# Softmax sums by half the products with ones: key tiles added in pairs on GpSimd, and value products moved among the thirds of Q and K

## The reference, cut to what matters

```
att = einsum('bhqd,bhkd->bhqk', q, k) * (1.0 / sqrt(hs))
att = where(causal, att, -inf)
att = softmax(att, axis=-1)
y = einsum('bhqk,bhkd->bhqd', att, v)
```

## Time and profile before

| what | value |
|---|---|
| median of three runs | 1278.62 us (1278.06 to 1281.37) |
| profiled execution, its time | 1269.57 us |
| its span | 1267.7 us |
| PE busy, share | 93% |
| DVE, ACT, POOL busy, share | 54%, 36%, 19% |
| mean granted clock of PE | 0.968 |
| M(1), first of the steps M that the change can move | 76.35 us |
| M(14) | 389.92 us |

### The profile page before, as it was taken

How to read it: one execution, slowest core, us unless ns; L and a number is a source line. 1 busy time by engine, 2 the same in 40 slices (tenths; PEclk the granted TensorE clock), 3 DMA queues, 4 the chain that set the end, 5 groups by cost and what they waited for, 6 DMA issues and landing times.

```text
span 1267.7 us, 20196 instructions
## 1 busy us (share of the span) xinstructions
PE 1183.1 (93%) x6404; PEld 935.7 (74%) x6404; DVE 686.9 (54%) x1469; ACT 456.2 (36%) x699; POOL 240.8 (19%) x370
## 2 busy tenths in 40 slices
PE   7788999999999879994999999999999999999996
PEld 5565676576575558883688888899999997778885
DVE  5564656656557546664447634343444442666744
ACT  3254435334435322222343334244444433333331
POOL 2021314413414410003100440000000000433200
PEclk8989999999999979997999999999999999999998
DMA  7336573532524222225223666245345531666440
GB/s 241 86 100 238 179 249 118 133 88 51 150 61 125 80 85 83 84 76 157 101 82 93 208 227 199 79 149 175 122 145 172 171 99 53 206 178 195 144 139 33
DMA packets 129277, 169.72 MB, mean 134 GB/s; under 512 B 17553, under 2 KB 70801, under 8 KB 129169
## 3 DMA queue, kind: packets, MB, share of 16 engines
q1 hardware_dynamic: 115360, 136.64, 35.2%
q0 software_dynamic: 8496, 28.32, 6.7%
q10 hardware_dynamic: 5312, 3.42, 1.2%
HBM read 95.98 MB, written 47.19 MB: 113 GB/s over the span
## 4 chain that ended last, share of the span: by engine, by line
PE 74%; DVE 8%; SPq 5%; POOL 3%; DMA 3%; issue 3%; ACT 2%; ACTq 1%; POOLq 0%; DVEq 0%
PE routed_ps L819 18%; PE routed_ps L1370 16%; PE psT L471 11%; SPq L354 5%; PE chosen_psG L819 4%; PE chosen_psY L819 4%; PE routed_ps L1389 2%; PE routed_ps L1390 2%; PE routed_ps L1391 2%; PE psS L537 2%; PE psO L576 2%; POOL routed_rows_io L1308 2%; PE psN L576 2%; PE psE L558 2%; PE routed_ps L1411 1%
## 5 line engine op out<-in xcount | busy, mean ns | idle before, releaser
L471 PE MATMUL psT<-store 128*128 128x512 f32 x576 | 157.2, 408 | 5.4 <-DVE store L685 3.5
L754 DVE CUSTOM_DVE_ANT_0 psS<-psS,attn_mask 128x512 f32<-128x512 f32 (+3 forms) x256 | 120.8, 510 | 60.3 <-PE psS L537 60.3
L641 ACT ACTIVATE acc<-psE 128x512 f32<-128x512 f32 x160 | 93.7, 599 | 141.7 <-PE psE L558 138.2
L1370 PE MATMUL routed_ps<-routed_later,routed_held 128*128 128x512 f32 x528 | 127.3, 398 | 3.6 <-issue 2.9
L1370 PE MATMUL routed_ps<-routed_first,routed_held 128*128 128x512 f32 x528 | 128.0, 396 | 1.4 <-DVE routed_first L1809 1.4
L471 PEld LDWEIGHTS psT<-store 128*128 128x128 f32 x576 | 105.7, 195 | 25.1 <-issue 4.0
L1370 PEld LDWEIGHTS routed_ps<-routed_later,routed_held 128*128 128x128 f32 x528 | 100.5, 192 | 28.0 <-DVE routed_held L1713 3.5
L819 PE MATMUL routed_ps<-routed_held,routed_h_hi 128*128 x624 | 116.1, 328 | 0.5 <-DVE routed_h_lo L1754 0.3
L1370 PEld LDWEIGHTS routed_ps<-routed_first,routed_held 128*128 128x128 f32 x528 | 99.7, 191 | 22.2 <-DVE routed_first L1809 1.8
L1308 POOL DMA_INDIRECT routed_rows_io<-sorted_y,routed_pos x32 | 37.6, 1175 | 387.8 <-DMA sorted_y<-routed_rows_io 314.0
L413 POOL TENSOR_SCALAR_AFFINE_SELECT acc<-acc 128x256 f32<-128x256 f32 (+1 forms) x160 | 57.2, 365 | 274.0 <-ACT acc L641 273.7
(11 more groups left out here) (249 smaller groups left out, 1973.8 us busy)
## 6 DMA issues: line engine op xcount, KB each, us to landing
sorted_x<-attn_zero SPq DMA_DIRECT2D x19, 768.0 KB, 5.9
routed_sraw<-in_L_ffn_Sg_dram SPq DMA_DIRECT2D x44, 256.0 KB, 3.1
routed_sraw<-in_L_ffn_Su_dram SPq DMA_DIRECT2D x44, 256.0 KB, 3.5
routed_sraw<-in_L_ffn_Sd_dram SPq DMA_DIRECT2D x44, 256.0 KB, 4.0
routed_rows_io<-sorted_x SPq DMA_DIRECT2D x39, 256.0 KB, 3.0
sorted_y<-routed_rows_io SPq DMA_DIRECT2D x39, 256.0 KB, 2.3
attn_qS<-attn_ch_hi SPq DMA_DIRECT2D x128, 64.0 KB
attn_kS<-attn_ch_hi SPq DMA_DIRECT2D x112, 64.0 KB
```

The source lines that it names most:

```text
L471: last = pe.matmul(out, lhs[a](k), rhs[c](k), start=(s[-1] == 0 and k == 0), stop=(s[-1] == 2 and k == KC - 1))
L641: act.activation(p_f[:, u, :], psE[:, n % 2, :], ACT.Exp, scale=SCALE).then_inc(exp_done, 1)
L754: last = dve.tensor_tensor_reduce(scores, scores, mask[:, (3 - t) * P:T], 1.0, BELOW_ALL, ALU.add, ALU.max, rowmax[:, g % 2, t, i:i + 1])
L1370: last = pe.matmul(out, w[:, slot, at + k * P:at + (k + 1) * P], x_part(k), start=(g == 0 and k == 0), stop=(g == 2 and k == KC - 1))
```

## The change

In the groups 0 to 12 (`in_sums`) the products of PV go to `psO` alone. GpSimd adds (AD) key tile 1 to the matching 384 columns of key tile 0, two heads at a time (parts 0 and 1, 768 columns each), and key tile 3 to the last 128 columns of key tile 2 (part 2, 512 columns), in place in `p_f`, behind the value products that read them. Two products with ones (RS 0 with 512 columns and RS 2 with 256) then give the sums. PV 0 moves ahead of the head; PV 1, 3 and 2 move among the thirds of K; AD 0 and 1 stand in the list behind the second and third third of Q, AD 2 and RS 0 behind the last PV, two P1 between RS 0 and RS 2. The exponentials of the next group wait for all of it. The ten P2 of a round stand behind RS 2, with five P1 among the first of them, and NORM's parts stand at the first three places there. Groups 13 to 15 stay as they were.

```diff
--- before.py
+++ after.py
@@ -19,6 +19,10 @@
 EPS = 1e-5
 ONE = 1
 BELOW_ALL = -1e30
+
+
+def in_sums(g, NG):
+    return g < NG - 3
 
 
 def attention_steps(B, QT, NG):
@@ -66,16 +70,30 @@
         p2 = [("P2", s, u) for u in range(10)]
         norm = [("NORM", s - 1, n) for n in range(3)] if s else []
 
+        summed = s and in_sums(s - 1, NG)
+        pieces = [("PV", s - 1, j) for j in order] if summed else []
+        if summed:
+            steps += pieces[:1]
         for n, one in enumerate(head):
             steps += [one] + left[n:n + 1] + (p1[n - 3:n - 2] if n >= 3 else [])
             if n == 3:
                 steps += [("M", s)]
+            if summed and n in (1, 2):
+                steps += [("AD", s - 1, n - 1)]
+            if summed and n >= 3:
+                steps += pieces[n - 2:n - 1]
+                if n == 3:
+                    if at == 3 and b and b < B - 1:
+                        steps += [("LZ", b)]
         if not head:
             steps += p1[:2] + [("M", s)]
             p1 = p1[2:]
         else:
             p1 = p1[3:]
-        if s:
+        if summed:
+            steps += [("AD", s - 1, 2), ("RS", s - 1, 0)] + p1[:1] + early[:1] + p1[1:2] + [("RS", s - 1, 2)] + early[1:]
+            p1 = p1[2:]
+        elif s:
             for n, j in enumerate(order):
                 steps += [("PV", s - 1, j)] + p1[n:n + 1] + p2[n:n + 1] + early[n:n + 1]
                 if s == NG - 2 and n < 2:
@@ -151,6 +169,12 @@
         if s[0] in ("XT", "CW") or (s[0] in ("Q", "K") and s[-1] == 2):
             hi_order[s[:-1] if s[0] in ("Q", "K") else s] = len(hi_order)
 
+    def pv_before(g):
+        return sum(QT + in_sums(n, NG) for n in range(g))
+
+    def pv_all(g):
+        return pv_before(g + 1)
+
     def first(s):
         return s[0] not in PARTS or s[-1] == 0
 
@@ -274,6 +298,7 @@
         exp_done = sem("exp_done")
         mask_done = sem("mask_done")
         pv_done = sem("pv_done")
+        sum_done = sem("sum_done")
         flip_done = sem("flip_done")
         norm_done = sem("norm_done")
         yh_done = sem("yh_done")
@@ -412,6 +437,18 @@
                     at = blocks[:, 0:1, :] if u < 4 else blocks[:, 0:4:3, :] if u < 8 else blocks[:, 0:4:2, :]
                     pool.affine_select(out=at, in_=at, compare_op=ALU.is_ge, fill=drop, base=0,
                                        pattern=[[0, at.shape[1]], [1, P]], channel_multiplier=-1).then_inc(mask_done, 1)
+                elif kind == "AD":
+                    g, part = s[1:]
+                    if part < 2:
+                        at, more_p = p_f[:, 2 * part:2 * part + 2, P:T], p_f[:, 4 + 2 * part:6 + 2 * part, 0:3 * P]
+                        pool.wait_ge(pv_done, pv_before(g) + 1)
+                        pool.wait_ge(mask_done, UNITS * g + 6 + 2 * part)
+                    else:
+                        at = p_f[:, 8:10, :].rearrange("p u (h n) -> p u h n", h=2)[:, :, :, P:2 * P]
+                        more_p = p_f[:, 4:8, 3 * P:T].rearrange("p (u h) n -> p u h n", h=2)
+                        pool.wait_ge(pv_done, pv_before(g) + QT)
+                        pool.wait_ge(mask_done, UNITS * (g + 1))
+                    pool.tensor_tensor(at, at, more_p, ALU.add).then_inc(sum_done, 1)
                 elif kind == "YH":
                     g = s[1]
                     pool.wait_ge(yh_done, g + 1)
@@ -570,12 +607,22 @@
                         if g % 4 == 0:
                             for i in range(QT):
                                 pe.wait_ge(sh_free[bank_of["V", g // 4, i]], use_of["V", g // 4, i] + 1)
-                    for to, values in ((psO, lambda i: v_f[:, j, (g % 4) * P + i * D:(g % 4) * P + (i + 1) * D]), (psN, lambda i: ones[:])):
+                    kinds = [(psO, lambda i: v_f[:, j, (g % 4) * P + i * D:(g % 4) * P + (i + 1) * D]), (psN, lambda i: ones[:])]
+                    for to, values in kinds[:1] if in_sums(g, NG) else kinds:
                         for i in range(4):
                             u, c0 = E_AT[j, i]
                             last = pe.matmul(to[i * D:(i + 1) * D, j * P:T], values(i), p_f[:, u, c0:c0 + (QT - j) * P],
                                              start=(j == 0), stop=(j == 2), tile_position=(0, i * D))
                     last.then_inc(pv_done, 1)
+                elif kind == "RS":
+                    g, j = s[1:]
+                    pe.wait_ge(sum_done, 3 * g + (2 if j == 0 else 3))
+                    for i in range(4):
+                        u, c0 = E_AT[j, i]
+                        last = pe.matmul(psN[i * D:(i + 1) * D, j * P:T], ones[:], p_f[:, u, c0:c0 + (QT - j) * P],
+                                         start=(j == 0), stop=(j == 2), tile_position=(0, i * D))
+                    if j == 2:
+                        last.then_inc(pv_done, 1)
 
         @block.scalar
         def _(act):
@@ -636,8 +683,11 @@
                     act.wait_ge(e_full, n + 1)
                     if u == 0 and g == 0:
                         act.wait_ge(w_lo_done, 5)
-                    if u in (0, 4, 8) and g:
-                        act.wait_ge(pv_done, QT * (g - 1) + {0: 1, 4: 3, 8: 4}[u])
+                    if g and in_sums(g - 1, NG):
+                        if u == 0:
+                            act.wait_ge(pv_done, pv_all(g - 1))
+                    elif u in (0, 4, 8) and g:
+                        act.wait_ge(pv_done, pv_before(g - 1) + {0: 1, 4: 3, 8: 4}[u])
                     act.activation(p_f[:, u, :], psE[:, n % 2, :], ACT.Exp, scale=SCALE).then_inc(exp_done, 1)
                 elif kind == "YH":
                     g = s[1]
@@ -757,7 +807,7 @@
                 elif kind == "NORM":
                     g, part = s[1:]
                     if part == 0:
-                        dve.wait_ge(pv_done, QT * (g + 1))
+                        dve.wait_ge(pv_done, pv_all(g))
                         dve.transpose(flip, psN[:]).then_inc(flip_done, 1)
                     elif part == 1:
                         dve.wait_ge(flip_done, 3 * g + 1)
```

## The result

The changed kernel takes 1312.3 us (median of 4 runs, 1309.7 to 1313.8); the kernel before, run beside it, takes 1278.3 (1270.7 to 1281.4). The ratio of the two is 1.027, with a 95% interval of 1.022 to 1.032: slower, by some 34 us, where I had forecast 15 and a range that ended at 1304. The sign was right, and so was the mechanism as far as it went; the size was not. The profiled execution has a span of 1307.2 us against 1267.7, and PE waits for other things than before. This is the view of what PE waited for between 80 and 440 us: total, times, longest.

What follows compares the result with a forecast made beforehand. Bare rounds were taken as bound by SP's loop of Q and K stack copies, 19.1 to 19.6 us; terms summed to +15.0, a span near 1283 and, with the median's offset added, 1293.6 us; range 1280 to 1304.

Steps and rivals of the forecast that it cites:

- the clock term: PE's clock drops after idle in bare-round tails, about 1.5 us lost each, mostly absorbed; 2.9 us added, bounds 0 and 8.
- clock and queue worse: Rival, chance 0.17: the clock falls in every bare tail unabsorbed, 7 x 1.5 = 10.5 us; total +22, 1301 us.
- Round 1: Four turns of x on DVE, 0.69 us each, lengthen this round to 22.8 from 20.8: +2.0 us.
- The tail of a bare round: Scores units behind RS2 wait for DVE in rounds without V or PR products; the round takes 20.2 us, not 17.8.
- GpSimd's queue: PV1 waits 1.3 us for masks behind ZB or scatters; rounds 7 and 11 lose 2.6 us together from this.
- The V wait: PV0 waits 0.95 us for the bias add of V's last third, three times, in rounds 5, 9 and 13.
- Rounds 4, 8, 12: V wait 0.95, masks 1.3 and RS0 0.4, less the saving of 0.64: +2.0 us each, +6.0 together.
- PV0 in round 0: The first PV0, moved in front of Q's thirds of round 1 where PE sets the pace, adds 1.2 us.
- Rounds 5 and 9: Rounds filled with V or PR products, where the net saving shows: -0.64 us each, -1.3 together.
- Rounds 2 and 3 have a loop of 21.2: SP's stack copies of Q and K plus four clears set these rounds at 21.2 us, so they lose nothing.
- M_6 to M_7: Time between the M steps of rounds 6 and 7, a bare round; 19.1 us before, near 20.2 predicted.
- The products with ones: Dropping those of key tiles 1 and 3 saves PE 0.91 us a group, 0.64 net of an extra block, 13 groups.

Runs made afterwards that it cites:

- the run with the stretch filled: Changed kernel plus unused 512-column products on PE, seven ahead of P1 number 8 and two ahead of number 9, in bare rounds; 1300.0 us, ratio 1.017.
- the late one: Changed kernel with NORM and round 1's last turns of x four slots later, value products and first two adds also later; 1276.0 us, ratio 0.9993.

## Why the prediction was wrong in size

**What failed.** The step is the clock term: "Lost would be about 1.5 in front of M", "I add 2.9, bounds 0 and 8". I had priced a drop by the one row that showed one, 118 to 120 us, as 1.5, and then let GpSimd's wait and the slack swallow most. The mechanism was right and named ("resembles it"), the size was not, and the argument that other waits and the slack would swallow most of it did not hold. Once down, the clock stays down for about 10 us (224 to 234), most of it dense work: the rest of the tail, PV0 and two of Q's three thirds. Against the run with the stretch filled, that is 3.5 us in rounds 6 and 10, 2.9, 2.7 and 3.0 in rounds 1 to 3, 1.5 in round 7, 0.2 in round 11 (there the filled run's clock fell too, behind a wait for masks). In rounds 4, 8 and 12 it is -1.3, for there the late PE no longer waits for masks. Over all rounds the two kernels differ by 12.4 us, by the medians 12.3. That is 9.5 over the term, 4.4 over its upper bound, and the largest single piece of the 19.7 by which the sum of rounds missed. The rival "clock and queue worse" had the drop in every bare tail, as it was, but at the same 1.5 each, and so stopped at 1301.

Round 1 needs a reserve. In the changed kernel its clock fell at about 91 us, ahead of the place of the filling, after waits of 1.56 and 1.44 for loads of x; in the filled run the same two waits (1.34 and 1.51) stand in the same code and the clock stayed at 1.00. So the 2.9 of round 1 are the price of a drop, but no run shows that the filling prevented it. The other 9.5 us remain, and they alone lie above the upper bound of 8.

The slack in rounds 2 and 3, my argument against that rival, was real but too small: with the clock up they are 20.6, 0.6 and 0.7 below the loop of 21.2 and 21.3; the drop costs 2.7 and 3.0 there, and +2.1 and +2.3 came through.

The page "TensorE: Matmul & The Clock Gate" of the Trainium skill (Part 1, "HAM oscillation") describes such a pattern: a stall brings the clock down, and the work behind it starts at half speed, again in each pass of the loop. The waits of its example are longer, about 3 to 5 us. Here the pass is a bare round and the stall 1.58 us, and the run with the stretch filled bears the pattern out with 12 us.

**The other terms**, by the run with the clock up, where they can be read:

- The tail of a bare round, "20.2 in place of 17.8": 20.6. In rounds 6 and 10 +1.5 each, predicted 1.1. Right within 0.4, which is the size of a wait for an exponential (0.40) in these tails; the 20.6 is an upper bound for the order alone, since the filling may take longer than the wait that it fills.
- GpSimd's queue, "a wait of 1.3": 1.2 to 1.74, five times. Right in place; in rounds 7 and 11 the longest ones (1.74, 1.57), and in round 11 the block behind it took 1.40 in place of 0.85, at the lower clock. These rounds came to +6.5, predicted +3.8.
- The V wait, 0.95: 0.87, three times. Rounds 4, 8, 12: +2.1 each, predicted 2.0. The sum is right by luck: it is the V wait (0.87) and the masks (1.2) alone. The 0.4 for RS 0 isn't there, and the saving of 0.64 isn't either: less its waits, such a round takes PE 28.0 us in both kernels.
- PV0 in round 0, +1.2: +1.1 in the changed kernel, but +1.7 in the filled run and +0.3 in the one without adds. Not settled: round 0 varies by more than that from run to run.
- Adds, 1.87 and 1.25. GpSimd's groups by form have 1829 and 1279 ns. Right. By the estimate from the page "GPSIMD Engine Reference" of the Trainium skill (section 3.1) it would have been 1.66 for 768 columns; the trace stands above it.
- Rounds 5 and 9, -0.64 each: +0.7 and +0.6. Wrong. At 202.55 the first product behind the new order waits 1.39 for a copy of DVE where it waited 0.66 before, and at 207.11 another 0.40 for an exponential. Its own work fell by about 0.5; it waited 1.1 more.
- Round 1, +2.0: +3.4 with the clock up. Two of the four turns of x now wait for their loads, 1.34 and 1.51 us there (1.56 and 1.44 in the changed kernel); the forecast priced DVE's work there and not the loads.
- Round 14, 0: +1.6 to +2.1, by a wait of 1.55 for a row maximum at 434.31 in a round whose order hasn't changed. In the run with adds in calm rounds alone it is 16.6 again. I have no cause for it that a run shows.
- Round 13, -1.8: -0.7 in both kernels, with one wait of 0.40 for an exponential. PE's own work fell by 1.1 of the 1.8.
- "Rounds 2 and 3 have a loop of 21.2": shown by the run with fewer copies. The same claim for rounds 6, 7, 10 and 11 was half right: M_7 to M_8 fell to 18.3, M_6 to M_7 stayed, behind DVE's normalisation.
- "The products with ones", 0.64 a group net: it depends on the order. In the late one PE's own work fell by 0.4 in rounds 2 and 3 (0.3 by M to M) and by 0.7 and 1.0 in rounds 8 and 9 (the two kernels with fewer copies). In the changed one it fell by less than 0.1 in rounds 4, 8 and 12 and by 0.5 in rounds 5 and 9. None of it came through, as forecast for the bare rounds; for the filled ones I had counted it in full.
- Two slips in the working: 1.07 + 5.2 + 0.36 is 6.63 and not 6.65, and the chance of slower, 0.78, is 0.02 more than its named parts can give. Neither moves the forecast.

Of the signs named, the halved products with ones, the long wait ahead of a P1 of 256 columns, the adds of 1.8 us, SP's pause and the V wait are there. The second P1 wait (0.8) is there in rounds 2 and 3, with 0.58 and 0.60, and absent in rounds 6, 7, 10 and 11, where PE, at half the clock, comes later than its maximum. The waits for masks are absent; M_6 to M_7 is 24.1 in place of 20.2 and M_7 to M_8 24.0 in place of 21.5.

## What to carry to other kernels

Price an idle stretch on PE not by its own length but by the dense work that follows it: here 1.58 us of waiting cost about 3 more in most bare rounds. When the clock is low, waits on other engines vanish from the list; keep PE busy once with products that nothing uses, and the list shows what the order costs by itself. And when work is moved out of a mixed stretch, look at what it leaves behind: twelve units of scores in a row ran at the pace of DVE, though PE had less to do.

## What the chip showed that I had not expected

- The clock fell after an idle stretch of 1.58 us whose surroundings were only part busy (PE 0.78 of 2 us in 222 to 224), and stayed at 1.2 GHz for 10 us, in the last six of which PE never paused. A wait of 1.36 ahead of M_7 in the kernel before with fewer copies left the products behind it at full speed.
- The length of a wait does not say whether the clock falls. In round 1 the kernel before waited 1.87 us (PE 0.20 of 2 us busy in 90 to 92) and stayed at 1.00; with fewer copies it waited 1.92 at the same place of PE's list and read 0.51 in 96 to 98. In 236 to 238 the kernel before had PE busy 0.55 of 2 us and stayed at 1.00 as well. So one row could give the price of a drop, but not how often to expect one.
- Half a clock hid other costs as well as making its own: the five mask waits, 7.0 us in the filled run, are absent from the changed kernel.
- An add of 768 columns of two inputs takes GpSimd 1.83 us and one of 512 takes 1.28. By a line through these two, an estimate, that is 2.1 ns a column and 0.18 us fixed.
